# Layer 1 keys and values as three float32r products, with operands split by GpSimd in the first attention

## The chip, the cores and the metric

The kernel runs on one core of a Trainium2 chip. The metric is device microseconds of one execution, lower is better. The engines named below are TensorE (PE in the profile, PEld its weight loads), VectorE (DVE), ScalarE (ACT), GpSimd (POOL) and the DMA queue issued by SyncE (SP).

## The reference

Two layers, each a cross attention and a feed-forward part, on `x` of 4 x 512 rows of 256 values, with a second input `ctx` of the same shape. Gates are tanh of given numbers. In outline, with layernorm in front of each part:

```python
# layer 0 attention: 16 heads of 16, a time bias, softmax, output product
Q = heads(n0 @ Wq.T + bq); K = heads(ctx @ Wk.T + bk); V = heads(ctx @ Wv.T + bv)
attn = softmax(Q @ K.T / 4 - 0.1 * |t - s|)
x = x + gate0 * ((attn @ V) @ Wo.T + bo)
# layer 0 feed-forward: weights rounded to -1, 0, 1
x = x + gate2 * (relu(n1 @ q(W1).T + b1) @ q(W2).T + b2)
# layer 1 attention
qp, kp, vp = relu(n2 @ Wq.T), relu(ctx @ Wk.T), relu(ctx @ Wv.T)
x = x + gate1 * softmax(qp @ kp.T / 4) @ vp
# layer 1 feed-forward: 4 experts, each row takes the one of its largest router value
x = x + gate3 * layernorm(gelu(n3 @ W1[e] + b1[e]) @ Wo + bo + n3)
```

The values must keep almost full float32 precision, since the router takes a maximum.

## The kernel before

The program is one hand-ordered list of instructions for each engine; semaphores tie them together, and nothing is reordered by a tool. `B` = 4 batches, `QT` = 4 tiles of 128 rows to a batch, `C` = 2 halves of the 256 columns. A head group is 4 heads of one batch; there are `G` = 16 groups for a layer. The stages that matter here follow each other in time:

1. Layer 0 projections (keys, values, queries of all batches).
2. The first attention, `attention(0)`. TensorE runs, for each group `g` and each key tile `k` (0 to 3), the five score products (L794), up to four products whose row maxima are needed two groups ahead (L680, reduced by VectorE at L1594), and `weigh` (L811), the product of the probabilities of the tile two steps earlier with the values. ScalarE takes the exponentials (L1142). GpSimd multiplies the diagonal block of each probability tile by a correction: `fix` (L1372), one for each `(g, k)`; `weigh` waits for it. After `fix(g, 0)` GpSimd does `split_maximum(0, g + 1)` (L1357, L1360, L1362): it negates the maxima of the next group and splits them into two parts. At `k` = 1 TensorE waits for that, after `weigh`, and transposes them (`turn_maximum`, L774); then it transposes the output of an earlier group (`turn_out`, L782). GpSimd's order inside a group is: fix 0, split of the next maxima, fix 1, fix 2, fix 3.
3. The middle stretch, four batches in a loop (`for b in range(B)`). TensorE: the keys of layer 1 (`project`, L596, plain float32, two output halves), the output product of layer 0's attention (`oproj`, L906, four tiles), the transposes of the next batch's attention rows (`turn`, L648; in the last batch `turn_n1(0)`, those of the normalised rows), the values of layer 1 (`values`, L607, plain float32). VectorE: `add_gated` for each of the four tiles, which is an add of the bias from PSUM into `tmp` (L1788) and a multiply-add of `tmp` into `x` (L1790); the tile's PSUM bank is free after the first. Then `variance(1, b)` (L1528, L1536, L1538), GpSimd's root (L1293), four small Newton steps (L1547 to L1553) and `normal(1, b)` (L1560). In batch 2 `quantise(0)` (L1780, L1782) stands between variance and normal, in batch 3 `rows0_low(0)` (L1828). After the loop comes `quantise(1)`, and then `rows0_low(1)`. GpSimd: `keys_low` (L1348) and the root of each batch.
4. Layer 0 feed-forward: TensorE's `up0` (L929) for 8 column blocks `f` of batch 0, with `turn_n1(1)` after `f` = 3; then for the next batches two `up0` and one `down0` (L943) by turns. `up0(b, 0)` waits for `rows0_low(b)`; `down0(0, 0)` waits for `quantise(1)` and for GpSimd's eight `hid_lo` subtractions of batch 0 (L1426), which follow the last root in GpSimd's order. Both halves of ScalarE's output (`hid0_full` has four buffers) feed those subtractions.
5. The second attention, and the experts' part.

Of the kernel before, what the change touches and what calls it, by code (L numbers as in the profile page):

```python
# [16 lines left out]
P = 128  # L17
# [106 lines left out]
def gated_blocks_program(nc, a, out):  # L124
    with ExitStack() as ctx:
# [36 lines left out]
        with ExitStack() as pro:  # L162
            with ExitStack() as inputs_:
                ctxT = sb("ctxT", [P, C, B * S], F32, inputs_)
            turned_x = sb("turned_x", [P, 2, C, S], F32, pro)
            hid_low = {"hi": sb("hid0_first_hi", [P, FC // 2, S], F32R, pro)}
            w_qkv = {"q": sb("w_q", [P, C, D], F32, pro)}
            with ExitStack() as parts_:
# [9 lines left out]
            with ExitStack() as rows_:  # L178
                xT = sb("xT", [P, C, B * S], F32, rows_)
            with ExitStack() as rows_:  # L180
                xT_hi = sb("xT_hi", [P, 2, C, S], F32R, rows_)
                xT_lo = sb("xT_lo", [P, 2, C, S], F32R, rows_)
# [35 lines left out]
        with ExitStack() as att:  # L218
            stack_q = sb("stack_q", [P, RING * 2 * S], F32R, att)
# [213 lines left out]

        def rows_of(b):
# [143 lines left out]
        def _(pe):  # L578
# [20 lines left out]

            def values(l, v):  # L600

                if l == 1:
                    wait(pe, sem(f"vals_read{l}"), v - 3)
# [79 lines left out]
            def first_maximum(l):  # L683

                raw_free(l, ("maximum", 0))
                pe.wait_ge(sem(f"max_split{l}"), 1)
                tr(raw_slot(l, ("maximum", 0))[0:2 * MP * PAIRS, 0:P], max_cols[:].bitcast(F32).rearrange("p i n c -> p (i n c)"), ident[:]
                   ).then_inc(sem(f"max_turned{l}"), 1)
# [64 lines left out]
            def attention(l):  # L753
# [16 lines left out]
                def turn_maximum(g):  # L770

                    score_free(("maximum", g))
                    pe.wait_ge(sem(f"max_split{l}"), g + 1)
                    tr(score_slot(("maximum", g))[0:2 * MP * PAIRS, 0:P],  # L774
                       max_cols[:].bitcast(F32).rearrange("p i n c -> p (i n c)"), ident[:]).then_inc(sem(f"max_turned{l}"), 1)

                def turn_out(g):

                    raw_free(l, ("out", g))
                    pe.wait_ge(sem(f"out_kept{l}"), g + 1)  # L780
                    for q in range(QT):
                        last = tr(raw_slot(l, ("out", g))[:, q * P:(q + 1) * P], out_rows[:, g % 2, q * P:(q + 1) * P], ident[:])  # L782
                    last.then_inc(sem(f"out_turned{l}"), 1)
# [17 lines left out]
                def weigh(n):  # L801
# [6 lines left out]
                    if k == 0:  # L808
                        wait(pe, sem(f"out_kept{l}"), g)
# [87 lines left out]
            for b in range(B):  # L897
                for c in range(C):
                    project(1, "k", b, c, context_of)
# [14 lines left out]
                for v in (2 * b, 2 * b + 1):  # L914
                    values(1, v)
# [153 lines left out]
        def _(act):  # L1069
# [33 lines left out]
            def turned_out(name, b):  # L1103
                for c in range(C):
                    u = b * C + c
                    act.wait_ge(sem(f"turned_{name}"), u + 1)
                    do(xT[:, c, b * S:(b + 1) * S], spare_banks[c][:] if name == "n0" else wide(u), ACT.Copy).then_inc(sem(f"turned_read_{name}"), 1)
# [9 lines left out]
            def keep_maximum(l, g):  # L1117

                n = 2 * MP * PAIRS
                act.wait_ge(sem(f"max_turned{l}"), g + 1)  # L1120
# [5 lines left out]
            def attention(l):  # L1126
                scores_done, exp_done, pv_done = sem(f"scores_done{l}"), sem(f"exp_done{l}"), sem(f"pv_done{l}")

                def keep_out(g):

                    act.wait_ge(pv_done, QT * HG * (g + 1))
                    wait(act, sem(f"out_turned{l}"), g - 1)
                    do(out_rows[:, g % 2, :], po[:], ACT.Copy).then_inc(sem(f"out_kept{l}"), 1)
# [179 lines left out]

# [709 lines left out]
```

## Time and profile before

| | |
|---|---|
| time before, median of 3 runs | 761.88 us (760.76 to 763.02) |
| the profiled execution | 764.34 us |
| its span from first to last instruction | 762.5 us |
| PE busy | 702.7 us, 92% of the span |
| DVE busy | 567.0 us, 74% |
| ACT busy | 451.4 us, 59% |
| POOL busy | 342.4 us, 45% |
| first attention | about 80 to 254 us of the span |
| middle stretch | 256 to 307 us |
| layer 0 feed-forward, batch 0's first products | 308 to 323 us |

The span is the time that the profile covers; some 1.8 us lie around it. Busy shares are averages over stages with different limits, so for a change in one stage the instructions of that stage are read in order of time. A matmul's shown duration includes its way through the array, so successive matmuls overlap in the rows; the pace of a series is the distance between starts, which the chain of waits shows as its merged time.

### The profile page before, as it was taken

The page shows a single profiled execution, that of the slowest core. Times are in us where ns is not written, and L with a number is a line of the kernel's source. Part 1 is how long each engine was busy: PE and PEld are TensorE (multiplying, and loading weights), DVE is VectorE, ACT ScalarE, POOL GpSimd, SP SyncE. Part 2 cuts the span into 40 slices and gives each one's busy share as a digit, 9 for nine tenths or more (in the row PEclk, how much of TensorE's full clock was granted, in tenths as well). Part 3 has the DMA queues.
Part 4 walks back from the last instruction along what each step waited for, and adds up shares of the span by engine and source line. Part 5 has one row for each costly group of instructions (what it writes and reads, how often), then busy time and mean ns, then how long its engine had stood idle before and what let it go on. Part 6 is the DMA issues. An engine that isn't in the chain of part 4 may idle for free.

```text
span 762.5 us, 12507 instructions
## 1 busy us (share of the span) xinstructions
PE 702.7 (92%) x4252; PEld 424.3 (56%) x4252; DVE 567.0 (74%) x1054; ACT 451.4 (59%) x968; POOL 342.4 (45%) x409
## 2 busy tenths in 40 slices
PE   5888999999999898899998999999999799999993
PEld 3444444444443466597763444444444488989983
DVE  5565899999992369555887999999997556766663
ACT  2322788888888453765514888888887234333330
POOL 3213455555555223754511020646652565755643
PEclk9999999999999999999999999999999989999997
DMA  7877645544555523102144255422201232211000
GB/s 224 229 247 170 195 159 178 192 165 159 178 183 191 162 60 111 43 1 70 35 135 112 71 179 188 140 75 85 86 2 58 88 109 92 76 37 51 26 16 15
DMA packets 51422, 87.53 MB, mean 115 GB/s; under 512 B 8662, under 2 KB 16856, under 8 KB 51361
## 3 DMA queue, kind: packets, MB, share of 16 engines
q1 hardware_dynamic: 43184, 71.39, 29.7%
q0 software_dynamic: 4640, 11.54, 5.0%
q10 hardware_dynamic: 3536, 3.81, 1.7%
q8 instruction: 35, 0.57, 0.3%
q14 instruction: 27, 0.21, 0.1%
HBM read 44.92 MB, written 41.63 MB: 114 GB/s over the span
## 4 chain that ended last, share of the span: by engine, by line
PE 60%; DVE 14%; POOL 12%; issue 7%; SPq 2%; ACT 2%; DMA 2%; POOLq 0%; DVEq 0%; ACTq 0%
PE ps_out L811 10%; PE ps_wide L680 7%; PE ps_out L1029 6%; PE ps_wide L1004 6%; PE ps_a L794 6%; PE ps_a L596 4%; PE ps_misc L794 3%; PE ps_a L929 3%; POOL w_lo L1312 3%; DVE rows_all L1560 2%; PE ps_a L1018 2%; PE ps_out L943 2%; DVE row_max L1594 1%; PE ps_wide L607 1%; SPq L495 1%
## 5 line engine op out<-in xcount | busy, mean ns | idle before, releaser
L1594 DVE TENSOR_REDUCE row_max<-ps_wide 128x2 f32<-128x1024 f32 x256 | 301.9, 1219 | 21.4 <-PE ps_wide L680 20.7
L1142 ACT ACTIVATE probs<-ps_a 128x512 f32<-128x512 f32 (+1 forms) x418 | 199.4, 523 | 28.0 <-PE ps_a L794 24.1
L680 PE MATMUL ps_wide<-stack_k,stack_q 48*128 48x512 f32 x512 | 145.2, 471 | 7.6 <-DVE row_max L1594 3.5
L794 PE MATMUL ps_a<-stack_q,stack_k 62*128 62x512 f32 (+3 forms) x418 | 137.9, 392 | 2.3 <-ACT probs L1142 1.8
L811 PE MATMUL ps_out<-probs,vals 128*17 128x512 f32 x1024 | 134.2, 598 | 0.5 <-POOL probs L1372 0.5
L1142 ACT ACTIVATE probs<-ps_misc 128x512 f32<-128x512 f32 (+1 forms) x222 | 114.2, 515 | 16.6 <-PE ps_misc L794 13.6
L1372 POOL TENSOR_TENSOR probs<-probs,fixes_sb 128x512 f32<-128x512 f32 x64 | 82.3, 1287 | 90.2 <-ACT probs L1142 90.2
L794 PEld LDWEIGHTS ps_a<-stack_q,stack_k 62*128 62x128 f32 (+1 forms) x418 | 63.6, 184 | 67.8 <-ACT probs L1142 31.2
L680 PEld LDWEIGHTS ps_wide<-stack_k,stack_q 48*128 48x128 f32 x512 | 68.5, 184 | 46.2 <-DVE row_max L1594 24.5
L794 PE MATMUL ps_misc<-stack_q,stack_k 62*128 62x512 f32 (+3 forms) x222 | 87.9, 396 | 1.3 <-ACT probs L1142 1.3
L794 PEld LDWEIGHTS ps_misc<-stack_q,stack_k 62*128 62x128 f32 (+1 forms) x222 | 40.9, 184 | 39.4 <-ACT probs L1142 30.5
L1276 ACT ACTIVATE hid1T_hi<-ps_a 128x512 fp32r<-128x512 f32 x38 | 20.7, 595 | 48.4 <-PE ps_a L1018 48.4
L1293 POOL TENSOR_TENSOR root<-var_eps,minus_half 128x4 f32<-128x4 f32 x16 | 17.6, 1097 | 68.2 <-DVE var_eps L1538 68.2
L1357 POOL TENSOR_SCALAR max_neg<-row_max 128x16 f32<-128x16 f32 x32 | 8.1, 254 | 87.4 <-DVE row_max L1594 87.3
L1267 ACT ACTIVATE hid<-ps_wide 128x512 f32<-128x512 f32 x38 | 22.7, 598 | 41.6 <-PE ps_wide L1006 41.6
L1029 PE MATMUL ps_out<-w_mo_hi,hid1T_hi 128*128 128x256 f32 x152 | 44.2, 291 | 1.3 <-DVE hid1T_lo L1903 1.3
L1029 PE MATMUL ps_out<-w_mo_hi,hid1T_lo 128*128 128x256 f32 x152 | 42.7, 281 | 0.0
L1029 PE MATMUL ps_out<-w_mo_lo,hid1T_hi 128*128 128x256 f32 x152 | 42.7, 281 | 0.0
L596 PE MATMUL ps_a<-ctxT,w_k 128*128 128x512 f32 x64 | 33.6, 670 | 7.9 <-DMA bias_qk<-in_L_bk 6.0
L1348 POOL TENSOR_TENSOR planes<-full,planes 128x512 fp32r<-128x512 f32 x16 | 20.3, 1269 | 44.7 <-ACT planes L1083 44.7
L1426 POOL TENSOR_TENSOR hid_lo<-hid_full,hid_hi 128x512 fp32r<-128x512 f32 x24 | 30.5, 1292 | 20.1 <-ACT hid_hi L1230 20.1
L811 PEld LDWEIGHTS ps_out<-probs,vals 128*17 128x17 f32 x1024 | 17.5, 95 | 33.3 <-POOL probs L1372 11.5
(246 smaller groups left out, 1344.2 us busy)
## 6 DMA issues: line engine op xcount, KB each, us to landing
rows_sorted<-blank SPq DMA_DIRECT2D x17, 1040.0 KB, 5.0
planes_k<-planes SPq DMA_DIRECT2D x32, 256.0 KB, 3.7
stack_k<-planes_k SPq DMA_DIRECT2D x64, 128.0 KB, 2.8
planes_q<-planes SPq DMA_DIRECT2D x32, 256.0 KB, 3.7
stack_q<-planes_q SPq DMA_DIRECT2D x64, 128.0 KB, 2.8
w_raw<-in_L_W SPq DMA_DIRECT2D x6, 1024.0 KB, 5.3
stack_k<-planes_k SPq DMA_DIRECT2D x64, 64.0 KB, 2.6
stack_q<-planes_q SPq DMA_DIRECT2D x64, 64.0 KB, 2.7
```

What stands on the lines that cost most here:

```text
L596: last = mm(proj_bank(l, s_, b, c), w_qkv[s_][:, k, c * P:(c + 1) * P], src(b)[:, k], start=(k == 0), stop=(k == C - 1))
L680: mm(raw_slot(l, ("pair", g, p))[:, i * S:(i + 1) * S], stack_q[at, slot(g, c) + q * P:slot(g, c) + (q + 1) * P], stack_k[at, slot(g, c):s ...
L794: mm(score_slot(("tile", n))[:, start:end], stack_k[at, slot(g, c) + k * P:slot(g, c) + (k + 1) * P], stack_q[at, slot(g, c) + start:slot( ...
L811: mm(po[32 * j:32 * j + VW, :], vals[:, k, g * HG + j, :], probs[n % PROBS[l]][:, j, :], start=(k == 0), stop=(k == QT - 1)).then_inc(sem( ...
L929: last = mm(ps[u % 2][:], w1_q[:, k, f * P:(f + 1) * P], rows[:, b % 2, k, :], start=(k == 0 and h == 0), stop=(k == C - 1 and h == 1))
L1004: mm(bank, sortedT[r][:, n % 2, c, :], w1_flat[w][:, bass.ds(at + (c * FF + half * S), S)], start=(i == 0 and c == 0), stop=False)
L1029: last = mm(po[:, 0:D], hid1T[r][:, n % 2, f, :], w_mo_part(w, f), start=(f == 0 and i == 0), stop=(f == FC - 1 and i == 2))
L1142: do(probs[n % PROBS[l]][:, j, start:end], score_slot(("tile", n * TILES + t))[:, start:end], ACT.Exp, scale=0.25).then_inc(exp_done, 1)
L1312: v.tensor_tensor(lo, raw, hi.bitcast(F32), ALU.subtract).then_inc(sem("w1_low"), 1)
L1372: v.tensor_tensor(block_, block_, fixes[:, k % 2, :].unsqueeze(1).broadcast_to([P, HG, P]), ALU.mult).then_inc(sem("fixed"), 1)
L1426: v.tensor_tensor(hidden0(b, "lo", f), hid0_full[:, u % 4, :], hidden0(b, "hi", f), ALU.subtract).then_inc(sem("hid0_low"), 1)
L1594: v.tensor_reduce(row_max[:, g % 2, :, p], raw_slot(l, ("pair", g, p))[:].rearrange("p (i k) -> p i k", i=2), AX, ALU.max).then_inc(sem(f" ...
```

## The change

- Layer 1's keys and values are no longer plain float32 products but the sum of three products of float32r parts (high x high, high x low, low x high), into the same PSUM accumulation (`keys1`, `values1`). The parts of `ctx` and of the two weights are made by GpSimd: a copy rounded to float32r, and a subtraction for the rest.
- GpSimd does that in the first attention, at the end of groups 2 to 9 (`split_context`, one 128x512 piece each) and 10 (`split_weights("k")`); `split_weights("v")` stands behind the attention.
- At the end of each group GpSimd also adds the gated output bias to one tile of `x`. VectorE's two instructions for a tile become one (`add_output`), which reads PSUM and `x`.
- VectorE's order for batches 2 and 3 changes: `normal(1, 2)` moves behind batch 3's four adds, and `rows0_low(0)` moves with it, both ahead of `variance(1, 3)`.
- The attention rows turned for `oproj` go to a buffer of their own (`att_rows`), since the parts of `ctx` now lie where `xT` is; some pairs of semaphores are merged into one that counts on.

```diff
@@ TensorE
+            def keys1(b, c):
+                if b == 0:
+                    pe.wait_ge(sem("ctx_low"), C * B + 1)
+                else:
+                    pe.wait_ge(*made(1, "k", "proj_high", b - 1, c))
+                for i, (r, w) in enumerate(PRODUCTS):
+                    for k in range(C):
+                        last = mm(ps[c][:], w_parts["k"][w][:, k, c * P:(c + 1) * P], context_parts(b)[r][:, k],
+                                  start=(i == 0 and k == 0), stop=(i == 2 and k == C - 1))
+                last.then_inc(made(1, "k", "proj_done", b, c)[0], 1)
+            def values1(v):
+                if v == 0:
+                    pe.wait_ge(sem("ctx_low"), C * B + 2)
+                wait(pe, sem("vals_read1"), v - 3)
+                for i in range(2):
+                    at = slice((2 * v + i) % QT * P, ((2 * v + i) % QT + 1) * P)
+                    for n, (r, w) in enumerate(PRODUCTS):
+                        for k in range(C):
+                            last = mm(vals_bank(1, v)[:, i * D:(i + 1) * D], context_parts(v // 2)[r][:, k, at], w_parts["v"][w][:, k, :],
+                                      start=(n == 0 and k == 0), stop=(n == 2 and k == C - 1))
+                last.then_inc(sem("vals_done1"), 1)
...
-                    project(1, "k", b, c, context_of)
+                    keys1(b, c)
...
-                        last = mm((po, pm)[t % 2][:, 0:D], xT[:, k, t * P:(t + 1) * P], w_o[:, k, :],
+                        last = mm((po, pm)[t % 2][:, 0:D], att_rows[:, b % 2, k, t % QT * P:(t % QT + 1) * P], w_o[:, k, :],
...
-                    values(1, v)
+                    values1(v)
@@ GpSimd
+            def split_context(n):
+                b, c = divmod(n, C)
+                hi, lo, raw = (z[:, c, b * S:(b + 1) * S] for z in (ctx_hi, ctx_lo, ctxT))
+                v.tensor_copy(hi, raw).then_inc(sem("ctx_high"), 1)
+                pool.wait_ge(sem("ctx_high"), n + 1)
+                v.tensor_tensor(lo, raw, hi.bitcast(F32), ALU.subtract).then_inc(sem("ctx_low"), 1)
+            def split_weights(s_):
+                n = C * B + "kv".index(s_) + 1
+                hi, lo = w_parts[s_]
+                pool.wait_ge(sem("w_layer1"), 16 * 3)
+                v.tensor_copy(hi[:], w_qkv[s_][:]).then_inc(sem("ctx_high"), 1)
+                pool.wait_ge(sem("ctx_high"), n)
+                v.tensor_tensor(lo[:], w_qkv[s_][:], hi[:].bitcast(F32), ALU.subtract).then_inc(sem("ctx_low"), 1)
...
                     if l == 0:
                         for k in range(1, QT):
                             fix(g * QT + k)
+                    if l == 0 and BEHIND <= g < BEHIND + C * B:
+                        split_context(g - BEHIND)
+                    if l == 0 and g == BEHIND + C * B:
+                        split_weights("k")
+                    if l == 0 and g == 0:
+                        pool.wait_ge(sem("gates"), 1)
+                        v.tensor_scalar(bias_o[:], bias_o[:], gates[:, 0:1], None, ALU.mult).then_inc(sem("bias_gated"), 1)
+                        pool.wait_ge(sem("bias_gated"), 1)
+                    if l == 0:
+                        v.tensor_tensor(x[:, g, :], x[:, g, :], bias_o[:], ALU.add).then_inc(sem("bias_added"), 1)
...
             attention(0)
+            split_weights("v")
@@ VectorE
+            def add_output(t):
+                dve.wait_ge(sem("bias_added"), t + 1)
+                dve.wait_ge(sem("oproj_done"), t + 1)
+                v.scalar_tensor_tensor(out=x[:, t, :], in0=(po, pm)[t % 2][:, 0:D], scalar=gates[:, 0:1],
+                                       in1=x[:, t, :], op0=ALU.mult, op1=ALU.add).then_inc(sem("oproj_tmp"), 1)
...
             for b in range(B):
                 for t in range(b * QT, (b + 1) * QT):
-                    add_gated("oproj", t, bias_o[:], 0)
-                dve.wait_ge(sem("oproj_added"), QT * (b + 1))
+                    add_output(t)
+                dve.wait_ge(sem("oproj_tmp"), QT * (b + 1))
+                if b == 3:
+                    dve.wait_ge(sem("turned_att"), C * b)
+                    normal(1, 2, x)
+                    rows0_low(0)
                 variance(1, b, x, 1e-5)
                 if b == 1:
                     thresholds()
                 elif b == 2:
                     quantise(0)
-                elif b == 3:
-                    rows0_low(0)
-                dve.wait_ge(sem("turned_att"), C * (b + 1))
-                normal(1, b, x)
+                if b != 2:
+                    dve.wait_ge(sem("turned_att"), C * (b + 1))
+                    normal(1, b, x)
             quantise(1)
```

## Rows read from the trace of the kernel before

**Rows 1.** The page's chain of work that ended last, shares by engine.
```profile
PE 60%; DVE 14%; POOL 12%; issue 7%; SPq 2%; ACT 2%; DMA 2%; POOLq 0%; DVEq 0%; ACTq 0%
```

**Rows 2.** Timeline of the first attention: start us, us, engine, line, operation [idle before].
```profile
189.25 1.29 POOL L1372 TENSOR_TENSOR probs<-probs,fixes_sb 128x512 f32<-128x512 f32 x1 [1.27 <-ACT probs L1142]
...
191.10 0.22 POOL L1362 TENSOR_TENSOR max_cols<-max_neg,max_cols 128x16 fp32r<-128x16 f32 x1
...
191.70 0.09 PEld L774 LDWEIGHTS ps_a<-ident_sb,max_cols 128*32 128x32 f32 x1 [0.85 <-ACT probs L1142]
```

**Rows 3.** GpSimd's groups of instructions: shapes, count, busy us, mean ns, idle before.
```profile
L1312 POOL TENSOR_TENSOR w_lo<-w_raw,w_hi 128x512 fp32r<-128x512 f32 x16 | 20.5, 1283 | 1.3
L1310 POOL CAST w_hi<-w_raw 128x512 fp32r<-128x512 f32 x16 | 9.8, 611 | 5.3 <-DMA w_raw<-in_L_W 5.3
L1300 POOL TENSOR_TENSOR rows_all<-rows_all 128x256 f32<-128x256 f32 x8 | 5.8, 726 | 0.7
```

**Rows 4.** The chain of waits, middle stretch: start us, us, what.
```profile
257.43 3.44 PE ps_a L596 x8
...
265.13 0.87 PE ps_wide L648 x8
266.01 3.46 PE ps_wide L607 x16
...
303.62 3.47 PE ps_wide L607 x16
```

**Rows 5.** The same chain, later: pace of float32r products.
```profile
329.35 1.86 PE ps_a L929 x8
331.20 1.89 PE ps_out L943 x16
```

**Rows 6.** VectorE adding the output: a group of the stretch, and one timeline row.
```profile
L1788 DVE TENSOR_TENSOR tmp<-ps_out,bias_o 128x256 f32<-128x256 f32 x8 | 3.4, 419 | 9.7 <-PE ps_out L906 9.7
...
262.33 1.28 DVE L1790 SCALAR_TENSOR_TENSOR rows_all<-tmp,gates,rows_all 128x256 f32<-128x256 f32 x1
```

**Rows 7.** Timeline of VectorE from batch 3's statistics on; the eighth `up0`'s last product.
```profile
303.81 1.41 DVE L1528 BATCH_NORM_STATS2 stats<-rows_all 128x6 f32<-128x256 f32 x4
...
305.67 0.17 DVE L1538 TENSOR_SCALAR var_eps<-meanvar 128x4 f32<-128x4 f32 x1
305.75 1.28 DVE L1828 TENSOR_TENSOR xT_lo<-ps_wide,xT_hi 128x512 fp32r<-128x512 f32 x2
...
307.82 1.38 DVE L1560 TENSOR_SCALAR rows_all<-rows_all,meanvar,rstd 128x256 f32<-128x256 f32 x4
...
310.44 3.41 DVE L1782 SCALAR_TENSOR_TENSOR w_q<-w_raw,quant,w_q 128x2048 fp32r<-128x2048 f32 x1
...
318.11 0.39 PE L929 MATMUL ps_a<-xT_lo,w_q 128*128 128x512 f32 x1
```

**Rows 8.** The chain of waits at the start of the feed-forward part.
```profile
307.76 1.21 PE ps_a L929 x4
...
310.40 7.08 POOL hid_first_lo L1426 x4
...
322.59 2.12 PE ps_out L943 x16
```

**Rows 9.** Timelines of GpSimd and VectorE, where a root is followed by subtractions.
```profile
340.37 1.01 POOL L1293 TENSOR_TENSOR root<-var_eps,minus_half 128x4 f32<-128x4 f32 x1 [2.42 <-DVE var_eps L1538]
341.35 5.15 POOL L1426 TENSOR_TENSOR hid_first_lo<-hid_full,hid_first_hi 128x512 fp32r<-128x512 f32 x4
...
341.51 1.27 DVE L1547 TENSOR_TENSOR newton<-root 128x4 f32<-128x4 f32 x1
```

**Rows 10.** TensorE behind an idle time; windows (engines' busy us, then PEclk).
```profile
611.29 1.94 PE L716 MATMUL ps_wide<-ident_sb,rows_all 128*128 128x128 f32 x8 [2.31 <-DVE picked L1638]
...
612.00:615.00 3.00, 3.00 (x15) 3.00 (x14) 0.25 (x1) 1.82 (x4) 2.53 (x4) 0.50 0.41 122
615.00:620.00 5.00, 5.00 (x32) 3.65 (x31) 1.13 (x2) 1.81 (x4) 4.30 (x6) 0.77 0.52 201
```

More of the change, by code:

```diff
@@ L164, in gated_blocks_program @@
                 ctxT = sb("ctxT", [P, C, B * S], F32, inputs_)
+            with ExitStack() as inputs_:
+                ctx_lo = sb("ctx_lo", [P, C, B * S], F32R, inputs_)
             turned_x = sb("turned_x", [P, 2, C, S], F32, pro)
@@ L167, in gated_blocks_program @@
             w_qkv = {"q": sb("w_q", [P, C, D], F32, pro)}
+            w_lo = {}
+            with ExitStack() as parts_:
+                for s_ in "kv":
+                    w_lo[s_] = sb(f"w_{s_}_lo", [P, C, D], F32R, parts_)
             with ExitStack() as parts_:
@@ L179, in gated_blocks_program @@
                 xT = sb("xT", [P, C, B * S], F32, rows_)
+            with ExitStack() as rows_:
+                ctx_hi = sb("ctx_hi", [P, C, B * S], F32R, rows_)
+                w_k_hi = sb("w_k_hi", [P, C, D], F32R, rows_)
             with ExitStack() as rows_:
@@ L218, in gated_blocks_program @@
         with ExitStack() as att:
+            with ExitStack() as s0:
+                att_rows = sb("att_rows", [P, 2, C, S], F32, s0)
+                sb("gap_stacks", [P, 2 * RING * S], F32, s0)
+                w_v_hi = sb("w_v_hi", [P, C, D], F32R, s0)
             stack_q = sb("stack_q", [P, RING * 2 * S], F32R, att)
@@ L432, in context_of, with context_parts @@
             return ctxT[:, :, b * S:(b + 1) * S]
+        def context_parts(b):
+            return ctx_hi[:, :, b * S:(b + 1) * S], ctx_lo[:, :, b * S:(b + 1) * S]
+        w_parts = {"k": (w_k_hi, w_lo["k"]), "v": (w_v_hi, w_lo["v"])}
         def rows_of(b):
@@ L772, in turn_maximum @@
                     score_free(("maximum", g))
[L773 removed]
+                    pe.wait_ge(sem("max_split"), l * G + g + 1)
                     tr(score_slot(("maximum", g))[0:2 * MP * PAIRS, 0:P],
[L775 removed]
+                       max_cols[:].bitcast(F32).rearrange("p i n c -> p (i n c)"), ident[:]).then_inc(sem("max_turned"), 1)
                 def turn_out(g):
                     raw_free(l, ("out", g))
[L780 removed]
+                    pe.wait_ge(sem("out_kept"), l * G + g + 1)
                     for q in range(QT):
                         last = tr(raw_slot(l, ("out", g))[:, q * P:(q + 1) * P], out_rows[:, g % 2, q * P:(q + 1) * P], ident[:])
[L783 removed]
+                    last.then_inc(sem("out_turned"), 1)
                 def scores(g, k, t):
@@ L808, in weigh @@
                     if k == 0:
-                        wait(pe, sem(f"out_kept{l}"), g)
+                        wait(pe, sem("out_kept"), l * G + g)
                     for j in range(HG):
@@ L1131, in keep_out @@
                     act.wait_ge(pv_done, QT * HG * (g + 1))
-                    wait(act, sem(f"out_turned{l}"), g - 1)
-                    do(out_rows[:, g % 2, :], po[:], ACT.Copy).then_inc(sem(f"out_kept{l}"), 1)
+                    wait(act, sem("out_turned"), l * G + g - 1)
+                    do(out_rows[:, g % 2, :], po[:], ACT.Copy).then_inc(sem("out_kept"), 1)
                 def weights(g, k, t):
@@ L1352, in split_maximum @@
             def split_maximum(l, g):
-                max_neg_ready, max_high = sem(f"max_neg{l}"), sem("max_high")
+                max_neg_ready, max_high = sem("max_neg"), sem("max_high")
                 pool.wait_ge(sem(f"max_done{l}"), PAIRS * (g + 1))
-                wait(pool, sem(f"max_split{l}"), g)
+                wait(pool, sem("max_split"), l * G + g)
                 v.tensor_scalar(max_neg[:], row_max[:, g % 2], -1.0, None, ALU.mult).then_inc(max_neg_ready, 1)
-                pool.wait_ge(max_neg_ready, g + 1)
-                wait(pool, sem(f"max_turned{l}"), g)
+                pool.wait_ge(max_neg_ready, l * G + g + 1)
+                wait(pool, sem("max_turned"), l * G + g)
                 v.tensor_copy(max_cols[:, :, 0, :], max_neg[:]).then_inc(max_high, 1)
@@ L1592, in maximum @@
                 if p == 0:
-                    wait(dve, sem(f"max_neg{l}"), g - 1)
+                    wait(dve, sem("max_neg"), l * G + g - 1)
                 v.tensor_reduce(row_max[:, g % 2, :, p], raw_slot(l, ("pair", g, p))[:].rearrange("p (i k) -> p i k", i=2),
```

17 lines of the change are left out of this document (9 added, 8 removed).

## The prediction

> **What bounds the kernel now.** I read the page's chain of waits first: 60% of it is TensorE's [rows 1], so an edit pays where TensorE's instruction list gets shorter or waits less, and costs where TensorE waits more. The change touches three stages, so I then read each by itself: the first attention in GpSimd's and TensorE's timelines, the middle stretch in the chain of waits, and the start of the feed-forward part in both.
>
> In the first attention TensorE runs without a gap, but one of GpSimd's results reaches it barely in time: the split maxima of the next group are ready at 191.10 + 0.22 = 191.32, and TensorE starts their transpose at 191.70 [rows 2]. That is 0.38 us of room, some 0.3 after a handover of 0.05 to 0.1. The 14 groups of the stretch from 84 us on show the same picture. In the middle stretch TensorE is the chain, with waits on VectorE's adds inside. At the start of the feed-forward part the chain goes through GpSimd's eight subtractions, from 310.40 on, the first four in 7.08 us, and `down0` starts behind the last, at 322.59 [rows 8].
>
> **The change part by part.**
>
> *GpSimd's additions in the first attention.* At the end of groups 2 to 10 stand a copy (0.61), a subtraction (1.28) and an add of 128x256 (0.73), by the same shapes elsewhere [rows 3]: 2.62 us, 2.67 with a handover. They stand behind fix 3, and the next fix, which starts at 189.25, finds GpSimd idle for 1.27 us until its exponentials are ready [rows 2]. So 1.27 us were free, and the next fix starts 1.40 late. The split maxima stand right behind it on the same engine and are 1.40 late too, against 0.3 of room. TensorE waits 1.1 us in each of 9 groups at `turn_maximum`; queued behind that wait are `turn_out`, the next scores, hence ScalarE's exponentials and VectorE's maxima. All of them are paced by TensorE, and nothing gives the time back: the next group starts in the same relation. The price is 9 x 1.1 = 9.9 us. The room could hide it all only if the additions took under 1.6 us; the rows leave 8.5 to 11. In the other groups only the bias add (0.73) is new, and 1.27 hide it. The fixes themselves are not the limit: TensorE's `weigh` stands two tiles of the group's 4 behind the scores that a fix belongs to. `split_weights("v")` (0.61 + 1.28) runs while TensorE ends the attention and turns rows, and the values are needed ten us later: nothing. What the fixes and the splits wait for otherwise is unchanged.
>
> *The products of the middle stretch.* Now a batch takes 3.44 for the keys, then `oproj` to 265.13, 0.87 for the transposes, 3.46 for the values, 257.43 to 269.47, 12.04 in all [rows 4]. `oproj` is 265.13 - 260.87 = 4.26 us, of which TensorE needs only four tiles of 0.87 (the transposes' and `oproj`'s first tile's time), 3.5: the rest is a wait for VectorE's adds, one of which takes 1.28 us [rows 6] because a GpSimd subtraction runs beside it. The new add reads PSUM, like the first of the two old ones, which takes 0.42 [rows 6] and isn't stretched anywhere; I take 0.42 to 0.5, under 0.87 either way, so the wait goes. Float32r products run at 1.86 / 8 = 0.2325 us for 512 columns and 1.89 / 16 = 0.118 for 256 [rows 5]. The keys become 12 x 0.2325 = 2.79, the values 24 x 0.118 = 2.83. A batch: 2.79 + 3.46 + 0.87 + 2.83 = 9.95. The stretch lasts from 257.43 to 303.62 + 3.47 = 307.09, 49.7 us; it becomes 4 x 9.95 + 0.34 for two small products = 40.1. Gain 9.5 us, of which 1.2 is batch 3, where VectorE's late normalisation held `oproj` up. It is 8 if the adds still stretch, 10 at best. ScalarE's list for a batch stays as it is and VectorE's gets shorter; that both keep up with 9.95 is an assumption (rival D).
>
> *VectorE's new order.* Let U be the start of `up0(0, 0)`, now 307.76 [rows 8]; it waits for ScalarE's last values. U now lies 307.76 - 302.75 = 5.0 behind the end of `oproj` (302.75 = 303.62 - 0.87 [rows 4]), and 4.4 with the shorter values. In that time VectorE has the end of the last add (0.5), Newton steps (from the variance's end to the normalisation pass 307.82 - 305.84 = 2.0 [rows 7]; less the root's 1.0 [rows 9] and handovers 0.8), the normalisation (1.38) and `rows0_low(0)` (1.28): 4.0, just hidden. But `variance(1, 3)` now comes behind it. It takes 305.84 - 303.81 = 2.0 us [rows 7] and ends at U + 1.7, where it now ends at U - 1.9. GpSimd's root ends at U + 2.8, and the next on GpSimd are the eight `hid_lo` subtractions, ready at U + 2.6 (310.40 - 307.76). So VectorE's Newton steps, which ran on an idle GpSimd until now, run beside them. What that does is in [rows 9]: root, four subtractions back to back to 346.50, and beside them the first of four Newton steps, 1.27 us long instead of 0.2, held until a subtraction ends; its three successors look the same, 1.2 each. By that pattern the steps end at U + 2.85 + 5.15 = U + 8.0. The normalisation (1.38, and one subtraction of 1.29 coming between) ends at U + 10.7; `quantise(1)` is 310.44 - 309.20 = 1.24 for L1780, which waits half a piece first and ends at U + 12.5, and 3.41 for L1782, in which a whole subtraction is waited for [rows 7]: U + 16.0; `rows0_low(1)` (1.28) at U + 17.3. `up0(1, 0)` waits for it, two of them take 1.86, and `down0(0, 0)` starts at U + 19.1, where it now starts at 322.59 - 307.76 = U + 14.8. Price 4.3 us. If nothing is held, `rows0_low(1)` ends at U + 10 and the price is 0; if a subtraction gets between all pieces, it is 6.
>
> The Trainium skill, "GPSIMD Engine Reference", section Specifications, says that GpSimd's SBUF interface is shared with VectorE and contended by VectorE instructions with two SBUF inputs or in a two-port mode. The trace agrees with that for the held Newton steps, and by the rule the new add, with one input in PSUM, is never held, which the sum above has anyway.
>
> *TensorE's clock.* TensorE would have nothing to do from about U + 10.7 (end of the eighth `up0`, now 318.50 [rows 7]) to U + 17.3. Behind an idle time of 2.31 us the granted clock is 0.50 for 612 to 615 and 0.77 on the mean for the five us after [rows 10], the lower of the two levels (1.2 GHz) for some 6 us of work, which costs 3. I take 2.0, since not all work behind the wait need fall into such a time; ends 0 and 3.5. For the attention's waits of 1.1 us I count none, since they are half as long.
>
> **The sum.** +9.9 - 9.5 + 4.3 + 2.0 = +6.7 us. The profiled execution took 764.34 (span 762.5) and gives 771.0; it lies 2.5 above the median of the runs shown, and against that median the sum is 761.88 + 6.7 = 768.6.
>
> **The rivals.**
>
> A. *VectorE isn't held in its new place.* The Newton steps could slip in ahead of the first subtraction (0.1 us decides) or find GpSimd idle. Then there is no late `rows0_low(1)` and no clock drop: +9.9 - 9.5 = +0.4, 762.3. Against it: [rows 9] has the very sequence. It decides from the point where the root ends before the first hidden tile is ready.
>
> B. *GpSimd's additions find room in the attention.* If the copies and adds were shorter beside idle neighbours than in [rows 3], or TensorE's wait were made up by a part that is in truth bound by VectorE, the 9.9 goes: 761.88 - 9.5 + 6.3 = 758.7. For it: VectorE is nearly full in that stage. Against: the chain there is TensorE's, and its room is 0.38.
>
> C. *Both A and B*, the faster side: the shorter products alone, 761.88 - 9.5 = 752.4.
>
> D. *The products aren't shorter*, because float32r parts stream no faster in this place, or VectorE's batch (its quantisation in batch 2 above all) becomes the bound: the gain falls to some 4 us, 774. Against it is the pace in [rows 5], the same shapes.
>
> **How the numbers follow.** Forecast 0.56 (766 to 772), A 0.14, B 0.10, C 0.10, D or a longer clock drop 0.10. The range from 758 to 774 takes in the forecast, A and B and leaves C and the far part of D out. A change of under 0.3% (2.3 us) can't be told from none. Faster is B and C: 0.2. Same is A, and a little of the forecast: 0.16. Slower is the rest: 0.64.
>
> **What would show it.** In the changed profile: TensorE idle for about 1.1 us ahead of the transposes L774 of groups 4 to 12 and a group period of 11.9 instead of 10.8 us there; a batch of about 10 us in the middle stretch, with no wait of `oproj` on VectorE; the Newton steps of batch 3 at 1.2 us each, `rows0_low(1)` some 17 us behind the first `up0`, and a granted clock below 1.00 behind it. I am wrong if the group period stays at 10.8, if those steps take 0.2 each, or if the batches stay above 11 us.

## Result, and the profile of the changed kernel

The changed kernel is slower: the median of four runs is 771.95 us (770.19 to 772.98) against 761.8 for the kernel before, and the ratio on record is 1.0104, 95% interval 1.0071 to 1.0136 (the two medians by themselves would give 1.0133). The kernel before took 763.3 to 763.6 us as median in the later sets of 23 to 27 runs; with 763.6 the ratio is +8 us (5.4 to 10.4). Two of the executions behind the ratios of this document, one of the kernel before and one with only the bias add moved, took over 1000 us and are left out of them. The forecast was 768.6 in a range from 758 to 774. The profiled execution took 770.19 (span 768.4), where the forecast had 771.0 for it.

The page's chain by engines, to set beside [rows 1]:

```profile
PE 51%; POOL 17%; DVE 13%; issue 11%; ACT 4%; DMA 2%; SPq 2%; POOLq 0%; DVEq 0%; ACTq 0%
```

TensorE's share of the chain fell from 60 to 51% and GpSimd's rose from 12 to 17%: work was taken from TensorE and given to an engine that then kept it waiting. Where, TensorE's waits say (engine, line, releaser: total us, times, longest):

```profile
PE ps_a L815 <- POOL max_cols L1423: 9.6, 10, 1.2
PE ps_a L970 <- DVE xT_lo L1907: 7.1, 1, 7.1
```

The first is the transpose of the split maxima: nine waits of 1.00 to 1.18 us in the first attention, and one of 0.29 us in the second, which the kernel before has too (0.3 in all there). The second is `up0(1, 0)` at the start of the feed-forward part; the kernel before has no such wait. GpSimd's timeline at the end of one loaded group of the first attention, with TensorE's transpose behind it, to set beside [rows 2] (start us, us, engine, line, operation, idle before):

```profile
145.32 1.28 POOL L1433 TENSOR_TENSOR probs<-probs,fixes_sb 128x512 f32<-128x512 f32 x1 [1.08 <-ACT probs L1186]
146.54 0.61 POOL L1362 CAST ctx_hi<-ctxT 128x512 fp32r<-128x512 f32 x1
147.23 1.28 POOL L1364 TENSOR_TENSOR ctx_lo<-ctxT,ctx_hi 128x512 fp32r<-128x512 f32 x1
148.48 0.74 POOL L1453 TENSOR_TENSOR rows_all<-rows_all,bias_o 128x256 f32<-128x256 f32 x1
149.17 1.29 POOL L1433 TENSOR_TENSOR probs<-probs,fixes_sb 128x512 f32<-128x512 f32 x1
...
151.03 0.22 POOL L1423 TENSOR_TENSOR max_cols<-max_neg,max_cols 128x16 fp32r<-128x16 f32 x1
...
151.40 0.27 PE L815 MATMUL ps_a<-ident_sb,max_cols 128*32 128x128 f32 x1 [1.01 <-POOL max_cols L1423]
```

No idle time is left ahead of the fix at 149.17, and the maxima end at 151.25; TensorE's transpose starts at 151.40 behind 1.01 us of idle. The fix behind the maxima stands at 127.37, 139.28 and 151.21 in three groups that follow each other: a period of 11.92 us, where the kernel before has 10.82. The group behind it took 13.27 (164.48 - 151.21), and there the windows show the lower clock for a few us:

```profile
154.00:156.00 2.00, 2.00 (x11) 0.53 (x5) 1.20 (x2) 0.82 (x2) 1.10 (x1) 0.50 0.01 3
156.00:158.00 2.00, 2.00 (x17) 1.09 (x13) 1.27 (x2) 1.82 (x5) 0.16 (x1) 0.72 0.00 0
```

The columns are the window, the busy us of TensorE, its weight loads, VectorE, ScalarE and GpSimd, then the granted clock, DMA share and GB/s: full TensorE at 0.50.

The chain of the middle stretch, a whole batch and the keys of the next, to set beside [rows 4]:

```profile
267.32 2.77 PE ps_a L626 x12
270.09 0.86 PE ps_out L947 x4
270.95 0.86 PE ps_misc L947 x4
271.81 0.94 PE ps_out L947 x4
272.76 0.86 PE ps_misc L947 x4
273.62 0.87 PE ps_wide L689 x8
274.49 2.85 PE ps_wide L639 x24
277.34 2.75 PE ps_a L626 x12
```

Keys 2.77 instead of 3.44, values 2.85 instead of 3.46, four tiles of the output projection in a row with no wait: 10.02 us a batch instead of 12.03.

The start of the feed-forward part, GpSimd, then VectorE, then the chain (to set beside [rows 7 to 9]). `up0(0, 0)` starts at 308.41.

```profile
310.02 1.01 POOL L1337 TENSOR_TENSOR root<-var_eps,minus_half 128x4 f32<-128x4 f32 x1 [7.05 <-DVE var_eps L1610]
311.05 5.03 POOL L1498 TENSOR_TENSOR hid_first_lo<-hid_full,hid_first_hi 128x512 fp32r<-128x512 f32 x4
```
```profile
311.13 1.23 DVE L1619 TENSOR_TENSOR newton<-root 128x4 f32<-128x4 f32 x1 [1.19 <-POOL root L1337]
312.40 1.21 DVE L1621 TENSOR_TENSOR newton<-newton,var_eps 128x4 f32<-128x4 f32 x1
313.64 1.22 DVE L1623 TENSOR_SCALAR newton<-newton 128x4 f32<-128x4 f32 x1
314.90 1.21 DVE L1625 TENSOR_TENSOR rstd<-newton,root 128x4 f32<-128x4 f32 x1
316.14 3.42 DVE L1632 TENSOR_SCALAR rows_all<-rows_all,meanvar,rstd 128x256 f32<-128x256 f32 x4
...
324.95 1.27 DVE L1907 TENSOR_TENSOR xT_lo<-ps_wide,xT_hi 128x512 fp32r<-128x512 f32 x2
```
```profile
326.28 3.78 PE ps_a L970 x8
330.07 2.47 PE ps_out L984 x16
332.53 1.86 PE ps_a L970 x8
```

The four Newton steps took 1.2 us each, one GpSimd subtraction apiece, and `down0(0, 0)` starts 21.66 us behind `up0(0, 0)`, where it was 14.83. The clock behind TensorE's 7.1 us of idle, in windows of the same columns:

```profile
322.00:324.00 2.00, 0.00 (x0) 0.00 (x0) 2.00 (x1) 0.00 (x0) 0.88 (x1) 0.50 0.00 0
...
326.00:330.00 4.00, 3.72 (x9) 2.95 (x10) 0.23 (x1) 1.26 (x2) 0.12 (x1) 0.50 0.01 2
330.00:332.00 2.00, 2.00 (x14) 2.00 (x13) 0.00 (x0) 1.26 (x2) 1.71 (x2) 0.70 0.00 0
```

A clock of 0.50 is the lower level, 1.2 GHz: the pair of `up0` products took 3.78 us instead of the 1.86 of the next pair.

For the comparisons below I cut the span at three points that every profile has: M, the first product of the second layer's keys; U, the first `up0`; D, the first `down0`. The times are the starts in the chain of waits, where a product that overlaps the one ahead of it counts from some 0.2 us later than in the timeline.

| kernel | M to U | U to D | M to D |
|---|---|---|---|
| before | 50.33 | 14.83 | 65.16 |
| changed | 41.09 | 21.66 | 62.75 |

So from M to D the change gained 2.4 us. Ahead of M it lost 9.9 us by the clock of the trace (257.43 to 267.32), and 11.4 counted from the start of the attention, which lay 1.55 us earlier in this execution (its first score product at 76.52 instead of 78.06). The windows show the likely reason: the clock fell to 0.50 between 54 and 56 us in both, and is 0.97 for 58 to 60 here, where the kernel before still has 0.50. 11.4 - 2.4 = 9.0, against the 5.4 to 10.4 of the runs. From D to the end of the span the changed kernel took 438.3 us, the kernel before 439.9. The kernels in which `down0` starts 18 us or more behind U took 436.4 to 438.9 us there (five kernels below and the changed one), the others 436.3 to 441.2 (six and the kernel before). An us or two of the late start may be made up there; the scatter hides it, and the medians decide.

### The profile page after: what moved, and what is told of

Same layout as the page of the kernel before. It is cut to its first block, busy times and chain, and to the rows that moved or that the text cites. A ratio compares the mean times of both kernels' runs of the same rounds, so it can differ in the third digit from the quotient of the medians.

```text
span 768.4 us, 12647 instructions
## 1 busy us (share of the span) xinstructions
PE 696.6 (91%) x4300; PEld 426.2 (55%) x4300; DVE 564.5 (73%) x1038; ACT 451.1 (59%) x968; POOL 370.8 (48%) x446
## 4 chain that ended last, share of the span: by engine, by line
PE 51%; POOL 17%; DVE 13%; issue 11%; ACT 4%; DMA 2%; SPq 2%; POOLq 0%; DVEq 0%; ACTq 0%
PE ps_out L852 7%; PE ps_out L1070 6%; PE ps_wide L1045 6%; PE ps_wide L721 4%; PE ps_a L835 4%; POOL probs L1433 3%; PE ps_a L970 3%; ACT probs L1186 3%; POOL w_lo L1356 3%; PE ps_a L614 2%; DVE rows_all L1632 2%; PE ps_misc L835 2%; PE ps_a L1059 2%; PE ps_out L984 2%; PE ps_a L626 1%
## 5 line engine op out<-in xcount | busy, mean ns | idle before, releaser
L1409 POOL TENSOR_TENSOR planes<-full,planes 128x512 fp32r<-128x512 f32 x16 | 20.3, 1270 | 39.7 <-ACT planes L1124 39.4
L1273 ACT ACTIVATE hid_full<-ps_a,b_cols 128x512 f32<-128x512 f32 x32 | 22.1, 690 | 27.4 <-PE ps_a L970 24.4
L970 PE MATMUL ps_a<-xT_hi,w_q 128*128 128x512 f32 x64 | 28.0, 438 | 9.0 <-DVE xT_lo L1907 7.1
```

What stands on the lines that cost most here:

```text
L970: last = mm(ps[u % 2][:], w1_q[:, k, f * P:(f + 1) * P], rows[:, b % 2, k, :], start=(k == 0 and h == 0), stop=(k == C - 1 and h == 1))
```

## Experiments

All ratios are to the kernel before, with their 95% interval; differences between kernels in us are differences of ratios times 763.6. The changed kernel has four runs, and its own interval is 2.5 us to either side, so small differences from it rest on the rows shown with them. The theory: (1) in the attention what costs is only that three GpSimd instructions stand ahead of the maxima, (2) in the feed-forward part that the last statistics come too late, so the Newton steps fall beside GpSimd's subtractions, (3) TensorE's idle time then halves its clock. The rivals: the attention is short of GpSimd or VectorE time as a whole; the late start is made up later; the clock fell for another reason.

**The splits behind fix 1.** The two instructions that split a piece are issued behind fix 1 of the same group instead of at its end. There the maxima that TensorE takes next are already split, and three fixes are still to come before the next split of maxima. The bias add stays at the end.

```
-                    if l == 0 and BEHIND <= g < BEHIND + C * B:
-                        split_context(g - BEHIND)
...
                             fix(g * QT + k)
+                            if k == 1 and BEHIND <= g < BEHIND + C * B:
+                                split_context(g - BEHIND)
```

> The changed kernel with the splits of groups 2 to 10 moved from the end of the group to behind fix 1, where GpSimd is idle for 2.1 us; the bias adds stay at the end. Deadline theory: the group period goes back from 11.9 to 10.8 us in all groups, the first attention gets 10 to 11 us shorter, and the time is 761 to 762 us (the start of the feed-forward part stays late). Load theory (GpSimd's additions slow the attention through shared resources wherever they stand): period stays near 11.9, 771 to 772 us.

Measured: 759.94 us, ratio 0.9952 (0.9928 to 0.9976). Same instructions, 11.6 us less than the changed kernel, and faster than the kernel before. GpSimd's timeline:

```profile
168.68 1.29 POOL L1433 TENSOR_TENSOR probs<-probs,fixes_sb 128x512 f32<-128x512 f32 x1 [0.46 <-ACT probs L1186]
169.93 0.60 POOL L1362 CAST ctx_hi<-ctxT 128x512 fp32r<-128x512 f32 x1
170.61 1.28 POOL L1364 TENSOR_TENSOR ctx_lo<-ctxT,ctx_hi 128x512 fp32r<-128x512 f32 x1
172.07 1.28 POOL L1433 TENSOR_TENSOR probs<-probs,fixes_sb 128x512 f32<-128x512 f32 x1 [0.19 <-ACT probs L1186]
...
175.66 0.73 POOL L1453 TENSOR_TENSOR rows_all<-rows_all,bias_o 128x256 f32<-128x256 f32 x1
176.96 1.29 POOL L1433 TENSOR_TENSOR probs<-probs,fixes_sb 128x512 f32<-128x512 f32 x1 [0.56 <-ACT probs L1186]
...
179.50 1.28 POOL L1433 TENSOR_TENSOR probs<-probs,fixes_sb 128x512 f32<-128x512 f32 x1 [0.46 <-ACT probs L1186]
```

A gap is left ahead of each fix shown, and the group takes 179.50 - 168.68 = 10.82 us as before. No wait of about 1 us is left at the transposes. The engine had the time; the place was wrong. The kernel before had the larger gap on show at this place, ahead of fix 2:

```profile
184.26 1.29 POOL L1372 TENSOR_TENSOR probs<-probs,fixes_sb 128x512 f32<-128x512 f32 x1 [2.10 <-ACT probs L1142]
```

M to D is 62.71, as in the changed kernel (62.75): the two stages don't touch each other.

**Only the bias add moved.** It goes behind fix 1, the splits stay. This tells a deadline (the lateness is what exceeds the room) from a price in proportion to the work.

```
+                            if k == 1 and g > 0:
+                                v.tensor_tensor(x[:, g, :], x[:, g, :], bias_o[:], ALU.add)...
...
-                    if l == 0:
+                    if l == 0 and g == 0:
```

> The changed kernel with only the bias adds (0.73 us) moved behind fix 1 from group 1 on; the splits (1.9 us) stay at the end of groups 2 to 10. Deadline theory: of what stands at the end, 1.27 us are idle time and 0.3 us room, so TensorE waits 1.95 - 1.27 - 0.3 = 0.35 to 0.4 us in each of 9 groups, period 11.2 us, and the time is 6.5 us under the changed kernel's: 765 to 766 us. A price in proportion to the added work (1.1 us for 2.67) would give 0.8 us in a group, period 11.6, and 769 us.

Measured: 764.92, ratio 1.0029 (0.9999 to 1.0059), 5.7 us under the changed kernel. The fixes behind the maxima stand at 161.60, 172.83 and 184.06, a period of 11.23. Taking 0.74 us of work out of the place takes 0.69 off the period, and TensorE's nine waits are 0.31 to 0.34 us long. The deadline holds, the proportional price (11.6) doesn't.

**The old order of VectorE for batches 2 and 3.** In the middle stretch the statistics of batch 3 stand ahead of its normalisation again, and batch 2 is normalised in its own turn.

```
-                if b == 3:
-                    dve.wait_ge(sem("turned_att"), C * b)
-                    normal(1, 2, x)
-                    rows0_low(0)
                 variance(1, b, x, 1e-5)
...
+                elif b == 3:
+                    rows0_low(0)
+                dve.wait_ge(sem("turned_att"), C * (b + 1))
+                normal(1, b, x)
```

> The changed kernel with VectorE's order for batches 2 and 3 as it was before the change (normal(1,2) right behind quantise(0), rows0_low(0) behind variance(1,3)). Held-steps theory: batch 3's Newton steps take 0.2 instead of 1.2 us, down0(0,0) starts some 15 us behind the first up0 instead of 21.7, no lower clock behind it; 1 to 2.5 us come back because oproj of batch 3 waits for VectorE: 766 to 768 us. Rival (the late start is GpSimd's eight subtractions in any case): 771 to 772 us, down0(0,0) still over 19 us behind the first up0.

Measured: 769.69, ratio 1.0086 (1.0057 to 1.0115), 1.4 us under the changed kernel with intervals that overlap, and above the 766 to 768 that I had expected. In the trace both ends moved: U to D is 14.88, the 6.8 us are back; but M to U is 45.43 instead of 41.09. VectorE's normalisation of batch 2 now ends at 305.1, and the last output projection waits for the adds behind it (chain of waits):

```profile
304.07 1.05 DVE rows_all L1632 x3
305.12 0.41 DVE rows_all L1861
...
305.57 2.08 PE ps_out L947 x4
307.65 1.40 PE ps_misc L947 x4
```

TensorE was idle for 2.62 us ahead of 305.57. The four-product tiles then took 2.08 and 1.40 instead of 0.86, at a granted clock of 0.50 for 306 to 308: some 1.8 us more. I had expected 1 to 2.5 us from this wait and got 4.3, which is the idle time and the clock together. The new order removes a real wait; it pays for it at the other end.

**GpSimd waits for the last normalisation.** `pool.wait_ge(sem("normed"), 2 * T)` ahead of the first `hid_first_lo`: the subtractions can't hold VectorE.

> The changed kernel, in which GpSimd also waits for the end of normal(1,3) before its first hid_lo subtraction. Held-steps theory: VectorE's four Newton steps take 0.2 us each, normal(1,3) 1.4 and ends some 5 us behind the first up0 (now 11.2), rows0_low(1) is done at about 11 us behind it (now 17.8), while GpSimd's subtractions start 2.3 us later and end at 18 to 19, so down0(0,0) starts 18.9 us behind the first up0 instead of 21.7: 768 to 770 us. Rival (the steps are slow for another reason, such as the shorter way to them): the steps still take 1.2 us and the time gets worse by 2 us or more, 774.

Measured: 768.79, ratio 1.0076 (1.0049 to 1.0102). U to D is 18.11, 3.55 less, though GpSimd's first subtraction starts 2.5 us later (313.56 against 311.05). VectorE's Newton steps, same instructions, same order:

```profile
311.25 0.16 DVE L1620 TENSOR_TENSOR newton<-root 128x4 f32<-128x4 f32 x1 [1.19 <-POOL root L1337]
...
312.05 1.38 DVE L1633 TENSOR_SCALAR rows_all<-rows_all,meanvar,rstd 128x256 f32<-128x256 f32 x4
```

0.16 instead of 1.23, and 1.38 instead of 3.42: what stretched them were GpSimd's subtractions. `down0` ran at the full clock (2.13). By the medians this is 2.1 us under the changed kernel, with intervals that overlap.

**TensorE kept busy.** The changed kernel, with 28 products that nobody reads ahead of the wait for the second batch's low part; nothing else differs.

```
             for b in range(B):
+                if b == 1:
+                    pe.wait_ge(sem("oproj_tmp"), T)
+                    ffn_going(po[:], 28)
                 pe.wait_ge(sem("rows0_lo"), C * (b + 1))
```

> The changed kernel with 28 products that nobody reads, ahead of TensorE's wait for the second batch's low part in the feed-forward (7.1 us of idle there, and half the clock behind it). If the idle is what took the clock, up0(1,0) and down0(0,0) to down0(0,3) run at the full clock and the kernel takes some 2.5 us less than the changed kernel: ratio to before 1.007. If the half clock has another cause or the time is hidden by the idle of later waits, the ratio stays at 1.010.

Measured: 769.04, ratio 1.0076 (1.005 to 1.0103), 2.1 us under the changed kernel, with intervals that overlap. VectorE's Newton steps are as late as there (309.47 1.24 and three like it), and the chain reads:

```profile
324.70 2.13 PE ps_a L970 x8
326.83 1.88 PE ps_out L984 x16
```

3.78 became 2.13 and 2.47 became 1.88: 2.2 us. The granted clock is 1.00 from 318 to 332. All four profiles with this idle time left empty have the drop, this one hasn't: the idle time was its cause. What it costs rests on the rows; the medians agree with it and don't prove it.

**The statistics early.** The splits behind fix 1, and each row block's statistics right behind its output addition, where VectorE waited for TensorE anyway; the aggregation behind the last.

```
                     add_output(t)
-                dve.wait_ge(sem("oproj_tmp"), QT * (b + 1))
+                    dve.wait_ge(sem("oproj_tmp"), t + 1)
+                    v.bn_stats(stats[:, t, :], x[:, t, :])...
+                aggregate(1, b, 1e-5)
...
-                variance(1, b, x, 1e-5)
```

> The splits stand behind fix(g, 1), as in e1_splits_moved, and in the middle stretch VectorE takes the statistics of each row block right behind its output addition, in the gaps in which it waited for TensorE. My theory is that after the late additions of the attention are gone, what is left of the loss is the late start of the feed-forward: the Newton steps of the last two batches run beside GpSimd's additions. With the statistics early they end before GpSimd starts, down0(0,0) then starts some 15 us behind up0(0,0) where the changed kernel had 21.7, at the full clock, and the kernel takes some 6 us less than e1_splits_moved: about 753.5 us, ratio to before 0.988. The rival, that the feed-forward hides its start (it catches up later, since TensorE waits there anyway), gives the 760 us of e1_splits_moved, ratio 0.995.

Measured: 755.34, ratio 0.9885 (0.9862 to 0.9908), 5.1 us under the first experiment and 8.8 under the kernel before. GpSimd's last root and its first subtractions:

```profile
297.83 1.10 POOL L1337 TENSOR_TENSOR root<-var_eps,minus_half 128x4 f32<-128x4 f32 x1 [2.79 <-DVE var_eps L1610]
303.82 7.47 POOL L1498 TENSOR_TENSOR hid_first_lo<-hid_full,hid_first_hi 128x512 fp32r<-128x512 f32 x4 [4.89 <-ACT hid_first_hi L1274]
```

The root ends 4.9 us before the first subtraction, so the new order costs nothing at its far end and the old one's wait isn't there either: M to U 41.87, U to D 15.16. The late start is not made up later, or this would have changed nothing. This is the version to keep.

**The splits moved and the old order.** The first experiment with the old order of the third.

> As e1_splits_moved, but with VectorE's old order for batches 2 and 3, as in e2_old_order. If the order does here what it did there (down0(0,0) 2.4 us earlier behind the start of the middle stretch, most of the gain eaten by products of the last batch that wait for VectorE), it takes 1.5 to 2.5 us less than e1_splits_moved: ratio to before about 0.993. If the old order alone were enough, it would reach e4_stats_early, 0.9885.

Measured: 758.83, ratio 0.994 (0.992 to 0.9959); M to U 45.41, U to D 14.88, the same two numbers as in the third. The order alone gives 0.9 us, with intervals that overlap (2.4 in the trace; I had expected 1.5 to 2.5), the early statistics 5.1.

**The products alone taken back.** The early-statistics kernel with plain float32 products for the second layer's keys and values and no low parts.

```
-                for i, (r, w) in enumerate(PRODUCTS):
-                    for k in range(C):
-                        last = mm(ps[c][:], w_parts["k"][w][:, k, c * P:(c + 1) * P], context_parts(b)[r][:, k], ...
+                for k in range(C):
+                    last = mm(ps[c][:], w_qkv["k"][:, k, c * P:(c + 1) * P], context_of(b)[:, k], ...
```

> As e4_stats_early, but the second layer's keys and values are again plain float32 products, and GpSimd makes no low parts: the three-part products alone are taken back. If they are worth what their groups show (keys 2.77 against 3.46 us, values 2.85 against 3.46 us, four batches), this takes 4 x 0.69 + 4 x 0.61 = 5.2 us more than e4_stats_early, ratio to before about 0.995. If the shorter products only turn into waits for VectorE or ScalarE, it takes no more than 1 us more.

Measured: 761.7, ratio 0.9972 (0.9953 to 0.999), 6.6 us more, where I had expected 5.2. M to U is 46.33, 4.5 us more, by keys of 3.43 and values of 3.46 us. The products are worth 4.5 to 6.6 us.

**The bias add alone taken back**, twice: in the early-statistics kernel and in the first experiment. The output addition is the old pair (`add_gated`), and GpSimd adds no bias.

```
-                    add_output(t)
+                    add_gated("oproj", t, bias_o[:], 0)
```

> As e4_stats_early, but the output addition is the old pair of instructions on VectorE and GpSimd adds no bias: the early bias alone is taken back. By the chain of the kernel before (0.42 to 0.49 us for each of the pair, each row block's product waiting for the one two before it) each batch of the middle stretch gets some 0.8 to 1 us longer: 3 to 4 us more than e4_stats_early, ratio to before about 0.993. The rival, that the pair costs nothing since VectorE has gaps, gives the same time as e4_stats_early.

> As e1_splits_moved, but the output addition is the old pair of instructions and GpSimd adds no bias; VectorE's order is that of the changed kernel. In e8_two_adds the statistics stood between the pairs and each batch took 11.2 us instead of 10.0. If the pair alone costs what the kernel before shows (four products of the output projection in 4.26 us instead of 3.5), a batch gets 0.8 us longer, and this takes some 3 us more than e1_splits_moved: ratio to before 0.999. If the pair costs 1.2 us a batch whatever stands between, it takes 5 to 7 us more: ratio 1.002 to 1.004.

Measured: 763.03, ratio 0.9983 (0.9964 to 1.0002), 7.5 us over its base, where I had expected 3 to 4; and 764.85, ratio 1.0028 (1.0003 to 1.0053), 5.8 us over its base, where I had taken 3 for a pair that costs 0.8 us a batch and 5 to 7 for one that costs 1.2. The batch takes 10.73 us in the second (257.81 to 268.54), 0.74 more than in its base, and 11.2 in the first, with statistics between the pairs. So the time came out as for 1.2 us a batch, and the batch as for 0.8. M to D is 3.5 us longer in the second and 6.5 in the first; what the second lost beyond 3.5 isn't located. Why the pair is long, VectorE's rows of the second show in the chain:

```profile
271.32 0.88 PE ps_out L947 x4
272.23 0.44 DVE tmp L1861
...
272.69 1.41 DVE rows_all L1863
274.10 0.35 DVE tmp L1861
...
274.49 1.13 PE ps_misc L947 x4
```

The second half of the pair, SBUF alone, took 1.41 us beside GpSimd's subtraction; the single addition, whose product comes from PSUM, took 0.48 at the same spot of the early-statistics kernel (273.13, with GpSimd's L1409 running from 271.96 to 274.63).

**TensorE kept busy ahead of the first `down0`.** The early-statistics kernel with 7 products that nobody reads in the last wait.

> As e4_stats_early, with 7 products that nobody reads in the 1.9 us in which TensorE waits for the last low part ahead of down0(0,0). In the profile of e4_stats_early down0(0,0) took 3.44 us at half the clock, in that of e7_plain 2.15 us at the full one, behind the same idle of 1.9 us; so the gain lies between nothing and 1.5 us: ratio to before 0.987 to 0.9885.

Measured: 755.49, ratio 0.9883 (0.9851 to 0.9915): no difference. Its `down0` took 2.16, that of its base 3.44 in the one profile that we have; that drop isn't in every execution, or it isn't worth what it seems. The runs don't tell which.

## Why the prediction was right, and where it wasn't

*The attention, +9.9.* Right in mechanism and place, and a little small. The forecast was 1.1 us in 9 groups; the trace has 11.92 - 10.82 = 1.10 in each of 9, TensorE's wait stands where it was put, and both experiments on the place fit the deadline. The whole stage lost 11.4 us in the profiled execution: the 1.4 beyond the sum is the group at the lower clock, behind one of the nine waits. The forecast had counted no clock for waits of 1.1 us; of the other three profiles with these waits (GpSimd held back, the old order, TensorE kept busy) none shows a granted clock under 1.00 between 86 and 258, so a drop there is an exception. Moving the splits gained 11.6. Rival B falls: nothing shortened the additions (0.61, 1.28, 0.74), and in the attention nothing gave the time back.

*The middle stretch, -9.5.* M to U fell by 9.24, with batches of 10.0 (forecast 9.95) and 40.4 us up to the 0.69 in which TensorE waits for the last values (forecast 40.1). The parts are sized less well than the sum. The products gave 4.5 where 4 x (0.65 + 0.63) = 5.1 stood. The pair of additions gave 3.4 (M to U 44.46 against 41.05), where the forecast had 4 x 0.80 = 3.2. The order had been credited with 1.2 us, for batch 3; against the old order under otherwise new conditions it is worth 4.3, because TensorE now reaches the last batch sooner and VectorE's normalisation doesn't, and because the lower clock behind the wait, which the forecast didn't count, is 1.8 of it. Taken back one at a time the parts cost 12.2 us in all and not 9.24, so they don't add up. Rival D falls with the pace of 2.77 and 2.85 us.

*The late start of the feed-forward part, +4.3, and the clock, +2.0.* U to D grew by 6.8 us, of which the half clock is 1.6, and it costs 0.4 more on `down0` itself: forecast 6.3, measured 7.2, made of 5.2 for the late start (4.3 forecast) and 2.0 for the clock (2.0). The steps of the list came out where they were put: the root's end at U + 2.6 (forecast 2.8), the Newton steps' end at U + 7.7 (8.0), `rows0_low(1)` at U + 17.8 (17.3). The experiment with GpSimd held back and the one with TensorE kept busy show both causes, each by itself. Rival A falls: the root ended at 311.03, the first subtraction started 0.02 us behind it and the first Newton step 0.10 us behind it, so the steps were too late by the very 0.1 us that the forecast had named.

*The sum.* +9.9 - 9.5 + 6.3 = +6.7 against +8 (5.4 to 10.4) in the runs: what is missing, an us or so, is within the interval. The 771.95 of the four runs lies above the 768.6 for one more reason, which isn't the change: the median that the forecast was set against, 761.88, came from three runs, and the later runs of the same kernel have 763.3 to 763.6. The prediction said that its sum ends at 771.0 for the profiled execution, which took 770.19. That these two lie so close is in part luck: in this pair of profiles the attention lost 1.5 us more than forecast and the stretch from M to D 0.8 more, and both are set off by an attention that began 1.55 us earlier and by a rest behind D that was 1.65 us shorter, neither of which was forecast.

What the prediction didn't see is that both losses were of place alone. It named the 1.27 us of idle time ahead of fix 0, in front of the maxima, and didn't look at the 2.1 us ahead of fix 2 behind them, and it listed the order of VectorE as old or new, not with the statistics cut into pieces. The same instructions in other places give 755.3.

## What to carry to other kernels

A helper engine that is half idle can still be full at one point: before giving it work, find the result of it that the bounding engine waits for soonest, and put the work right behind that result, not ahead of it. When the order of an engine's work is changed to remove a wait, follow each instruction that slides later to what it then runs beside; cutting it into the gaps ahead (statistics block by block) can be worth more than either order. Price a change by parts before keeping or dropping it whole: here the products were worth 4.5 to 6.6 us and the early bias 5.8 to 7.5, hidden under the 11 and 7 us that misplaced work cost.

## What the runs showed of the hardware

- Short VectorE instructions beside back-to-back GpSimd subtractions of 128x512 took 1.21 to 1.23 us instead of 0.16, and so did the `TENSOR_SCALAR` with its single tensor (1.22, L1623). By the Trainium skill, "GPSIMD Engine Reference", section Specifications, that takes two SBUF inputs or a two-port mode; whether this one was in such a mode no row shows. The addition with an input in PSUM was not stretched (0.48), which agrees with that section.
- TensorE's clock was 0.50 behind 7.1 us of idle in each of the four profiles that had it (`up0` pair 3.78, 3.78, 3.78 and 3.76 us), and stayed at 1.00 where products that nobody reads filled it. It was 0.50 behind 2.6 us of idle in both experiments with VectorE's old order and behind 2.7 us in the one with two adds and early statistics, and around an idle time of 2.1 us where GpSimd was held back. Behind 1.9 us it fell in one profile (`down0` 3.44) and not in another (2.15), and of the nine waits of about 1 us in the attention one was followed by 0.50 in one profile, none in three others. So for these shorter ones the length of the idle time alone doesn't say whether the clock falls.
